# Products of the identity issued on TensorE where it would wait, in a graph and attention kernel

## The reference

```python
# 1 graph attention: x1 = relu(n @ W_ah + b); three layers, all on x1, of 4 heads of 192
h = (x1 @ W).reshape(N, 4, 192)
e = leaky_relu(as_n[src] + ad_n[dst], 0.2)
alpha = softmax of e over the edges of each dst
out = segment_sum(alpha * h[src], dst) + b          # relu; three concatenated @ W_out, relu
# 2 mixture of 8 experts, the best 2 of each row
# 3 adapter and two graph convolutions with edge_weight
# 4 attention of 12 heads of 64, whose V comes from a recipe over basis matrices, then a
#   feed-forward block of 384:
Q = n @ q_w + q_b;  K = n @ k_w + k_b
attn = softmax(Q K^T / 8)
context = mean(attn) @ ctx_pat.T;  recipe = top-8 softmax of semantic * sigmoid(context)
V = (recipe-weighted n @ basis_A) @ vout_w + vout_b
x = x + attn @ V @ ao_w + ao_b;  x = x + gelu(ln(x) @ up_w + up_b) @ down_w + down_b
```

## Time and profile before

| | us |
|---|---|
| median of 3 runs | 3399.17 |
| lowest, highest | 3391.48, 3400.55 |
| the profiled execution | 3393.07 |
| its span | 3391.3 |
| TensorE (PE) busy | 2654.1 (78%) |
| VectorE (DVE) busy | 2014.4 (59%) |
| ScalarE (ACT) busy | 1358.2 (40%) |
| GpSimd (POOL) busy | 354.3 (10%) |

### The profile page before, as it was taken

One profiled execution on the slowest core, in us unless ns is written; L12 is line 12 of the kernel. 1 busy time (PEld: TensorE's weight loads), 2 busy tenths in 40 slices (PEclk: granted clock), 3 DMA queues, 4 the chain that ended last, 5 costly groups with the idle time before them and its releaser, 6 DMA issues. The chain is left out here.

```text
span 3391.3 us, 40509 instructions
## 1 busy us (share of the span) xinstructions
PE 2654.1 (78%) x14722; PEld 2336.5 (69%) x14723; DVE 2014.4 (59%) x2944; ACT 1358.2 (40%) x2206; POOL 354.3 (10%) x309
## 2 busy tenths in 40 slices
PE   6666596976976978994899559779796897999777
PEld 5555486876876867883798527467565675888776
DVE  7665457967967963225656415442795454888754
ACT  1223255655756642101566300031695102666420
POOL 1233021012003000000233102000000000111100
PEclk9988797988988988996999769979897896999978
DMA  0010311110111116211899730123561212334214
GB/s 31 15 30 16 87 38 36 54 61 36 54 61 36 53 37 147 55 28 46 277 258 260 187 78 1 46 89 125 132 133 26 92 45 46 80 85 96 56 37 96
DMA packets 107207, 268.25 MB, mean 79 GB/s; under 512 B 10894, under 2 KB 49280, under 8 KB 105806
## 3 DMA queue, kind: packets, MB, share of 16 engines
q1 hardware_dynamic: 99440, 239.43, 26.0%
q0 software_dynamic: 7616, 26.74, 3.6%
HBM read 195.58 MB, written 66.73 MB: 77 GB/s over the span
## 5 line engine op out<-in xcount | busy, mean ns | idle before, releaser
L840 PE MATMUL ps<-h,e_gat_aggregate 125*125 125x193 f32 x2400 | 408.6, 334 | 89.5 <-DVE e_gat_aggregate L824 73.4
L840 PEld LDWEIGHTS ps<-h,e_gat_aggregate 125*125 125x125 f32 x2400 | 402.0, 192 | 96.2 <-DVE e_gat_aggregate L824 77.1
L786 ACT ACTIVATE e_gat_aggregate<-row_gat_aggregate,from_src 125x1250 f32<-125x1250 f32 x120 | 160.7, 1339 | 166.6 <-PE ps L840 139.1
L103 PE MATMUL ps<-gat_w_pair_gat_scores,x_turned 128*125 128x384 f32 x1080 | 196.6, 344 | 39.1 <-DVE gat_w_pair_gat_scores L698 38.7
L822 DVE TENSOR_TENSOR e_gat_aggregate<-e_gat_aggregate 125x1250 f32<-125x1250 f32 x120 | 175.2, 1460 | 86.9 <-DMA gat_bias_gat_aggregate<-in_gat_b 47.8
L103 PEld LDWEIGHTS ps<-gat_w_pair_gat_scores,x_turned 128*125 128x125 f32 x1080 | 194.3, 190 | 41.1 <-DVE gat_w_pair_gat_scores L698 39.9
L314 PE MATMUL ps<-dst_hot_build_adjacency,src_hot_build_adjacency 125*125 125x128 bf16 x2380 | 186.7, 235 | 44.0 <-DVE dst_hot_build_adjacency L267 43.3
L314 PEld LDWEIGHTS ps<-dst_hot_build_adjacency,src_hot_build_adjacency 125*125 125x125 bf16 x2380 | 170.4, 148 | 70.1 <-DVE dst_hot_build_adjacency L267 56.7
L2233 DVE TENSOR_TENSOR p_low_attend<-p_attend,p_high_attend 125x1254 fp32r<-125x1254 f32 x120 | 184.2, 1537 | 45.6 <-ACT p_high_attend L2219 42.8
L103 PE MATMUL ps<-w_pair_dense_rows_from,col_dense_rows_from 128*125 128x384 f32 x1080 | 208.4, 352 | 1.8 <-DVE col_dense_rows_from L962 1.8
L266 DVE TENSOR_SCALAR src_hot_build_adjacency<-ode_iota_build_adjacency,_columns_build_adjacency 125x1250 bf16<-125x1250 f16 x238 | 134.9, 567 | 111.6 <-PE ps L314 75.5
(11 more groups left out here) (367 smaller groups left out, 5061.3 us busy)
## 6 DMA issues: line engine op xcount, KB each, us to landing
stock<-in_moe_w SPq DMA_DIRECT2D x34, 1152.0 KB
row_gat_aggregate<-r_scratch SPq DMA_DIRECT2D x24, 625.0 KB, 6.5
V_home<-q_scratch SPq DMA_DIRECT2D x48, 312.5 KB, 6.5
rows_dense_rows_from<-node_scratch SPq DMA_DIRECT2D x10, 1080.0 KB
stock<-in_gat_w SPq DMA_DIRECT2D x4, 2304.0 KB, 8.5
q_scratch<-V_home SPq DMA_DIRECT2D x6, 1250.0 KB, 4.6
k_scratch<-V_home SPq DMA_DIRECT2D x6, 1250.0 KB, 4.5
V_home<-k_scratch SPq DMA_DIRECT2D x24, 312.5 KB, 6.5
```

Of the source, the lines that this page charges most:

```text
L103: last = pe.matmul(out, left(x), right(y), start=start and n == 0, stop=stop and n == 2)
L786: a.activation(e[:, n % 3, 0, :], row[0:TP, head % 2, 0, :], ACT.Exp, bias=from_src[:, head, t:t + 1])
L840: last = pe.matmul(ps[0:TP, bank(head, d // 2), d % 2 * (C + 1):(d % 2 + 1) * (C + 1)], e[:, n % 3, 0, d * TP:(d + 1) * TP], h[:, t, head, :],
```

## The change

A helper `keep_busy` issues a number of f32 products of the 128x128 identity with itself, repeated four times along the columns (512 columns), into a bank of PSUM. Each starts its own sum, so nothing is accumulated. It waits for nothing and signals nothing. It is called at thirteen places of TensorE's lists: with 4 products at the head of `dense_turned`, 3 at the head and 3 at the end of `gat_scores`, 12 at the head and 10 at the end of `gat_aggregate`, 6 at the head of `dense_rows_from` and 7 after its first tile is turned, 16 at the head of `attention_statistics`, 8 at the head of `choose_recipes` and 11 before it turns the chosen weights, 16 at the head of `attend`, 7 at the head of `attended_product` and 6 at the head of `last_product`. As the stages run, that is 177 products in one execution. No other engine's list changes.

```diff
@@ -102,6 +102,14 @@
+def keep_busy(pe, g, bank, products):
+    ident = g["ident"]
+    for _ in range(products):
+        pe.matmul(g["ps"][:, bank, :], ident[:], ident[:].unsqueeze(1).broadcast_to([128, 4, 128]), start=True, stop=True)
@@ dense_turned
         def _(pe):
+            keep_busy(pe, g, 0, 4)
             for m in range(mt):
@@ gat_scores
         def _(pe):
+            keep_busy(pe, g, 0, 3)
             for t in range(NT):
...
             last.then_inc(r_turned, 1)
+            keep_busy(pe, g, 1, 3)
@@ gat_aggregate
         def _(pe):
+            keep_busy(pe, g, 0, 12)
             for head in range(HEADS):
...
                     last.then_inc(p_used, 1)
+            keep_busy(pe, g, 5, 10)
     ph.end()
@@ dense_rows_from
+            keep_busy(pe, g, 7, 6)
             for t in range(2):
                 for q in range(groups):
                     turn(t, q)
+                if t == 0:
+                    keep_busy(pe, g, 7, 7)
@@ attention_statistics
         def _(pe):
+            keep_busy(pe, g, 0, 16)
             for head in range(QH):
@@ choose_recipes
         def _(pe):
+            keep_busy(pe, g, 7, 8)
             pe.wait_ge(rn_ready, 1)
...
             last.then_inc(semantic_turned, 1)
+            keep_busy(pe, g, 7, 11)
             pe.wait_ge(f3, 1)
@@ attended_product
         def _(pe):
+            keep_busy(pe, g, 0, 7)
             for t in range(NT):
@@ last_product
         def _(pe):
+            keep_busy(pe, g, 0, 6)
             pe.wait_ge(w_split, 1)
```

## The result

| | us |
|---|---|
| median of 6 runs, changed | 3423.28 (3419.79 to 3425.24) |
| median of 6 runs, before | 3398.03 (3391.48 to 3400.55) |
| ratio, 95% interval | 1.0076 (1.0063 to 1.0089) |
| profiled execution, span | 3423.89, 3422.2 |

The change costs about 26 us, 0.76%. The forecast was 11.8 us slower, 3408 in 3394 to 3422: the direction was right, the size was less than half, and the measured time lies just above the range.

A forecast was written before the change was run, and what follows sets the result against it. The prediction took TensorE's waits at stage openings, and the low clock after them, as the bound. Overruns of 20.0 us less gains of 8.2 made it 11.8 us slower, forecast 3408 us, range 3394 to 3422.

The forecast's parts named there:

- Only the time after the opening can be filled: At stage openings, products are issued after the opening, so only the wait until the first matmul can hold them.
- price 0.94 and 1.72 us: Claimed cost of one product on TensorE: 0.94 us at the upper clock level, 1.72 at the lower.
- a rise of about 4.5 us: A run of products starting at the low clock stays slow for about 4.5 us, then runs fast.
- two records: Each product, as an ordinary f32 matmul, leaves two records in the trace.
- The overruns cost 20.0: Products outlasting waits in dense_turned, attended_product, choose_recipes' head, attention_statistics and attend lose 20.0 us together.
- gat_scores of layers 2 and 3 gain 3.2: Products at the end and head fit their waits; clock gain 4.7 us, less pause losses, leaves 3.2.
- gat_aggregate gains 3.0: Its twelve opening products fit in three layers; clock gain 6.5 us, less 0.5 and 3.0 charged, net 3.0.
- dense_rows_from gains 1.0: Products before and within the turns of rows fit TensorE's idle time; gain between 0 and 3 us, taken as 1.0.
- last_product: nothing: Its six products change nothing, since the second addition waits for a load; without this cover, some 3 us cost.
- Rival 1: Across pauses in the three layers the clock holds, and delays are short: even, 3393 to 3399 us; chance 20%.
- Rival 2: Products are too thin to raise the clock anywhere: some 121 us slower, 3514 to 3520; chance 5%.
- rival 3: A product leaves one record, costing 0.47 or 0.86 us: some 15 us gained, 3378 to 3384; chance 6%.

The follow-up runs named there:

- e2: The changed kernel without the products of dense_turned, attention_statistics, attend, attended_product, last_product and the eight at the head of choose_recipes; 3401.95 us, ratio 1.0008.
- e3: e2 without the three products at the head of gat_scores as well; 3395.9 us, ratio 0.9992.
- e8: The changed kernel, loop kept, with counts sized to the waits and none in dense_turned or at the heads of gat_scores and choose_recipes; 3398.26 us, ratio 0.9993.
- e6: The kernel before with only the three products at the head of gat_scores; 3399.73 us, ratio 1.0002.
- e16: The kernel before with only four products, hidden in a wait at the head of the first layernorm_turned; 3403.3 us, ratio 1.0018.
- e12: The kernel before with the changed kernel's products in gat_scores and gat_aggregate only, the layers still looped on the chip; 3405.82 us, ratio 1.0027.
- e18: The kernel before with only the twelve and ten products of gat_aggregate, none in gat_scores, layers looped; 3386.49 us, ratio 0.9976.
- e17: The changed kernel with four more products, hidden at the head of the first layernorm_turned; 3414.02 us, ratio 1.0055.
- e10: The kernel before with the three layers written out and products in gat_scores and gat_aggregate only; 3398.81 us, ratio 1.0.
- e5: The changed kernel with every product over 24 rows of the identity instead of 128; 3528.6 us, ratio 1.038.

## Why the prediction was wrong, by its steps

- *Only the time after the opening can be filled; price 0.94 and 1.72 us; a rise of about 4.5 us; two records.* Right, with the price 0.08 us too high at the upper level. The groups took 6.5 us for 4 (forecast 5.8), 9.1 for 7 (8.6), 8.9 for 8 (9.6), 16.6 and 16.1 for 16 (17.1).
- *The overruns cost 20.0.* Right as a sum: the stages named grew by 9.5 (dense), 3.9, 0.8, 2.0 and 2.7 us, 18.9. The runs gave 23, but e2 also lost the dense products that place the loop's head badly, some 6 to 7 us, which leaves 16. choose_recipes grew by 0.8 with both of its groups; with the eleven alone it took 53.0 (e2, e3) and 54.5 us (e8), and 52.7 to 54.3 in the kernels with no product there. So the eleven gain 1 us at most (forecast 1.0), and the eight cost 1 to 2 (forecast 3.6). The 2.0 of attend is smaller than that stage's own spread.
- *gat_scores of layers 2 and 3 gain 3.2.* This is the step that failed. They lost 6.9 and 7.5 us in the trace, 14.4 in all. The step read the 3.4 us between the opening and the first matmul as a wait that three products fit into. TensorE spends that time in its branch, so the products start behind it, at the lower level, and are all delay. Three more things stood against the step. The opening is paced by the split of the weights, so the high clock had nothing to give. The products at the end hold up the barrier, which the forecast charged in the first layer only, with 0.5. And the dense products moved the loop's head to where TensorE stops a second time. By the traces the head alone costs these two stages 6.1 us (e6), the placement alone 5.9 (e16) and the barrier 2.9 in the changed kernel, 14.9 against the 14.4. The runs put all six products of a layer at 17 (e12 against e18) and the placement at 6 to 7 (e16, e17).
- *gat_aggregate gains 3.0.* 2.5 in the trace, with the pause charged as it came; 8 us alone in e18, 5.6 on the mean of the traces. If anything too careful.
- *dense_rows_from gains 1.0.* 4.3 us in this trace, but that is mostly chance: on the mean it took 268.5 us in the eight traces with 128-row products in it and 269.8 in the eleven without, a gain of 1.3. No run has it alone.
- *last_product: nothing.* It took 1.2 us less, close.
- Rival 1 (no fall of the clock at the pauses) would not have saved the forecast: e10 has the clock up at both openings of `gat_scores` and the time of before. Its sum of 15.9 is also too low: it shortens the rise to 3.3 us but gives back the gains of a rise of 4.5; with both at 3.3 it is 18.8. The Trainium skill's rule on pauses (TensorE: Matmul & The Clock Gate, "Why this matters for your kernels") did not always hold: a pause of 2.0 us was followed by the low level. The same trace has nine pauses of 2.02 us inside `gat_aggregate`, and three of them were followed by it. Rival 2 came true in e5 alone, with 24 rows, and rival 3 nowhere: there are 354 records.

The forecast sum was 11.8. With the measured sizes it is 16 for the overruns, 17 for the six products, 6.5 for the placement, less 8 for `gat_aggregate` and 1.3 for the rows: 30, against 26 measured. The parts come from different runs, each within some 5 us, so the sum agrees no better than that.

What stays open: the stage `experts` has no product in it and took 320.2 us against 313.3, but it took 311.8 to 322.8 us over all the kernels here, with no pattern that follows a change. The two profiled executions differ by 31 us and the medians by 25, a surplus of about that size. And only e16 and e17 separate the number of TensorE's instructions from what they do, so in every other difference here the placement may have a part.

## What to carry to other kernels

Filling a wait with dummy products pays only if they end before the wait does and if what follows runs at TensorE's pace. Check both: the time from the stage's opening to the first real matmul, and who paces the first tile. Ahead of a barrier they are free only where another engine arrives later than they end, as with the ten at the end of `gat_aggregate`. At the head of a long hardware loop, find out first when TensorE really starts. And where a change adds instructions ahead of a hardware loop, read the loop's opening in the new trace, since part of the difference may be their number alone; a twin like e16, the same number of instructions where they are hidden, tells it.

## What the runs showed of the hardware

- TensorE's branch back to the head of the loop of layers cost 3.3 to 3.9 us in every looped kernel, and 0.08 us where it was not taken. Its branches in the short loops of the first stage took 0.20 to 0.26 us, and the other engines' branches at the same loop of layers 0.05 to 0.08. The table of waits names whatever semaphore the next matmul would have needed; only `<-issue`, once a matmul that waits for nothing stood there, gave it away.
- A second stop of 2.9 to 4.5 us from load to load comes or goes with the number of instructions ahead of the loop (e16, e17).
- A table load of 1.28 us on ScalarE stands at each opening of `gat_scores` in every looped kernel and in none with the layers written out.
- Twelve products over 24 rows, 20.81 us without a pause, left the clock at 0.50 (e5). With 128 rows it rose 3.5 us after the products began in the first gat_aggregate, 5.6 in the first dense stage and 5.2 in the statistics.
- Of nine pauses of 2.02 us inside `gat_aggregate` of the kernel before, three were followed by 3.4 us at the lower level.
